# The front of a gated cross-attention and mixture-of-experts kernel, with keys and queries merged into one product of raw inputs

## The reference, cut to what matters

```python
# x (4, 256, 256), ctx (4, 256, 64); 1024 tokens in all
kv   = ctx @ W_k.T + b_k                                   # per batch (256, 64)
out  = einsum('bij,bjd->bid', layernorm(x), kv)            # queries
sim  = einsum('bid,bjd->bij', out, kv) / 16
sim  = (sim - mean) * rsqrt(var + 1e-6) * ln_gamma + ln_beta
x    = x + tanh(g_xattn) * softmax(sim)
h    = layernorm(x)
# router: sigmoid(h @ gate.T), 2 of 4 groups by their two best, 4 of 16 experts, weights normalised * 2.5
x    = x + tanh(g_ffn) * (sum over experts w * (silu(h@gw.T) * (h@uw.T)) @ dw.T  + shared expert)
```

## Time and profile before

| | us |
|---|---|
| median of 3 runs | 198.45 |
| lowest, highest | 196.81, 202.37 |
| the profiled execution | 198.22 |
| its span, first to last instruction | 196.4 |

### The profile page before, as it was taken

The page is one execution under the profiler, slowest core; times in us unless marked ns, Lnnn a source line. Parts: engine busy times, 40 slices in busy tenths (PEclk is TensorE's granted clock), DMA queues, the critical chain, the costliest instruction groups (busy, mean ns, idle before and its releaser), DMA issues.

```text
span 196.4 us, 2883 instructions
## 1 busy us (share of the span) xinstructions
PE 185.1 (94%) x809; PEld 142.9 (73%) x809; DVE 147.1 (75%) x332; ACT 82.6 (42%) x164; POOL 82.6 (42%) x101
## 2 busy tenths in 40 slices
PE   7899799969899999999999989999999999999992
PEld 5565477847588888887788767888888888888871
DVE  0759968999899599998569999856676656666563
ACT  2448724523337833345466343343434343434210
POOL 2352161731832655553336434344445544445300
PEclk9999969999999999999999999999999999999999
DMA  6967200001775446632121000222211122111403
GB/s 154 331 191 228 72 0 0 0 0 34 242 213 176 150 135 164 170 123 53 53 53 53 3 0 18 98 76 76 63 53 53 57 78 76 56 53 53 160 0 110
DMA packets 10264, 18.06 MB, mean 92 GB/s; under 512 B 1741, under 2 KB 3789, under 8 KB 10254
## 3 DMA queue, kind: packets, MB, share of 16 engines
q1 hardware_dynamic: 9760, 17.37, 28.9%
q10 hardware_dynamic: 494, 0.57, 1.3%
HBM read 16.82 MB, written 1.11 MB: 91 GB/s over the span
## 4 chain that ended last, share of the span: by engine, by line
PE 69%; DVE 18%; DMA 6%; ACT 2%; issue 2%; DVEq 0%; POOL 0%; SPq 0%
PE bank L792 40%; PE bank L836 21%; DMA xs<-x_in 3%; DVE act_hi L556 2%; DVE act_lo L564 2%; DMA w_row<-weight_rows 2%; DVE bank L559 2%; PE bank L869 2%; PE bank L739 2%; PE bank L722 1%; DVE stats L461 1%; DMA weight_rows<-w_blk 1%; DVE beats L600 1%; PE bank L762 1%; PE bank L805 1%
## 5 line engine op out<-in xcount | busy, mean ns | idle before, releaser
L281 POOL TENSOR_TENSOR w_lo<-w_raw,w_hi 128x256 fp32r<-128x256 f32 (+1 forms) x72 | 72.0, 1018 | 77.3 <-ACT w_hi L324 76.3
L324 ACT CAST w_hi<-w_raw 128x256 fp32r<-128x256 f32 (+2 forms) x72 | 36.5, 513 | 55.5 <-PE bank L836 29.5
L792 PE MATMUL bank<-hT_hi,w_hi 128*128 128x512 f32 x142 | 56.5, 398 | 0.0
L792 PE MATMUL bank<-hT_lo,w_hi 128*128 128x512 f32 x142 | 56.3, 397 | 0.0
L792 PE MATMUL bank<-hT_hi,w_lo 128*128 128x512 f32 x142 | 44.6, 396 | 0.0
L538 DVE TENSOR_TENSOR weighted<-bank,w_row 128x512 f32<-128x512 f32 x30 | 20.7, 689 | 25.6 <-ACT bank L383 25.3
L792 PEld LDWEIGHTS bank<-hT_hi,w_lo 128*128 128x128 f32 x142 | 26.7, 188 | 6.4
L792 PEld LDWEIGHTS bank<-hT_hi,w_hi 128*128 128x128 f32 x142 | 26.7, 188 | 6.4
L792 PEld LDWEIGHTS bank<-hT_lo,w_hi 128*128 128x128 f32 x142 | 26.7, 188 | 6.1
L383 ACT ACTIVATE bank<-bank 128x512 f32<-128x512 f32 x30 | 17.5, 582 | 27.5 <-PE bank L792 27.5
L564 DVE TENSOR_TENSOR act_lo<-bank,act_hi 128x512 fp32r<-128x512 f32 (+1 forms) x37 | 25.0, 677 | 3.6
(11 more groups left out here) (104 smaller groups left out, 139.7 us busy)
## 6 DMA issues: line engine op xcount, KB each, us to landing
w_row<-weight_rows SPq DMA_DIRECT2D x31, 256.0 KB, 3.2
w_raw<-w_in SPq DMA_DIRECT2D x18, 384.0 KB, 3.8
xs<-x_in SPq DMA_DIRECT2D x4, 256.0 KB, 6.1
out<-x SPq DMA_DIRECT2D x4, 256.0 KB, 2.8
cw<-ctxw_in ACTq DMA_DIRECT2D x1, 276.2 KB
vec<-vecs_in ACTq DMA_DIRECT2D x1, 265.0 KB, 5.9
weight_rows<-w_blk SPq DMA_DIRECT2D x4, 16.0 KB
gw<-route_in ACTq DMA_DIRECT2D x1, 16.0 KB, 6.3
```

Source lines behind the costliest of these rows:

```text
L281: nc.gpsimd.tensor_tensor(w_lo[:, par, cols], w_raw[:, bass.ds(n, 1), cols].rearrange("p o c -> p (o c)"), w_hi[:, par, cols].bitcast(F32) ...
L324: nc.scalar.copy(w_hi[:, par, cols], w_raw[:, bass.ds(n, 1), cols].rearrange("p o c -> p (o c)"))\
L792: last = nc.tensor.matmul(dst, w[:, par, w0 + c * P:w0 + (c + 1) * P], m, start=i == 0, stop=i == len(parts) - 1, skip_group_check=True)
```

## The change: what it does

Queries and keys are no longer formed. With `square` = [W b]^T [W b], the score of a row of x and a context position is, up to the row's own scale and shift (which the normalisation of the scores removes), x times the context rows (`gathered`), times `square`, times the centred context (`projected`). The raw x is loaded a second time, already transposed. `offset` takes the mean key out, `centre_context` centres the context. For batches 0 and 1 GpSimd multiplies u by gamma and TensorE makes a second, scaled score product (`similarity_gamma`); for batches 2 and 3 VectorE multiplies by gamma (`sim_scale`). The variance of x enters only the small constant under the root (`row_eps`). The layer norm of x, its transposes and its copies go. The loads are cut into pieces and reordered. All copies out of PSUM in the front, other than `square`, are on ScalarE. The shared slices' gate and up products are taken batch by batch, those of batch 0 ahead of batch 1's hidden state.

```diff
 # SP
-            for b in range(B):
                 sp.dma_start(xs[:, 2 * b:2 * b + 2, :], x_v[:, 2 * b:2 * b + 2, :]).then_inc(x_in[b], 16)
...
+            load_rows(0, 1, rows0_in)
+            load_xT(0)
+            load_x(0)
+            load_xT(1)
+            load_x(1)
+            load_slice(0, 0)
+            load_slice(1, 1)
+            load_xT(2)
+            load_xT(3)
+            load_x(2)
+            load_x(3)
 # GpSimd
-            for b in range(B):
-                root(0, b)
+            pool.wait_ge(vec_in, 16)
+            u_times_gamma(0)
+            u_times_gamma(1)
+            root(1, 0)
+            root(1, 1)
             pool.wait_ge(gwhi_ready, 1)
...
             low_gu(0, 0, 0)
-            root(1, 0)
-            root(1, 1)
-            pool.wait_ge(scaled_ready, 1)
-            nc.gpsimd.tensor_tensor(x1[:, 3, :], prob[:, 3, :], xs[:, 3, :], ALU.add).then_inc(x1_ready[1], 1)
+            low_gu(1, 1, 1)
             root(2, 0)
             root(2, 1)
             pool.wait_ge(hid_ready[1], 2)
             low_d(0, 0, 0)
-            low_gu(1, 1, 1)
             root(1, 2)
 # ScalarE: queue, then work
-            act.dma_start(cw[:], ctxw).then_inc(ctxw_in, 16)
+            act.dma_start(wk[:], wk_aug).then_inc(wk_in, 16)
+            load_context(0, 1, cT0_in)
+            load_context(1, 2, cT1_in)
+            act.dma_start(rows[:, 1, :, :].rearrange("p c e -> p (c e)"), ctx_rows[:, 1, :]).then_inc(rows1_in, 16)
             act.dma_start(vec[:], vecs.partition_broadcast(P).rearrange("p o v -> p (o v)")).then_inc(vec_in, 16)
+            load_context(2, B, cT_in)
+            act.dma_start(rows[:, 2:B, :, :].rearrange("p b c e -> p b (c e)"), ctx_rows[:, 2:B, :]).then_inc(rows_in, 16)
             act.dma_start(gw[:], route_w.rearrange("(c p) e -> p c e", p=P)).then_inc(gw_in, 16)
...
+            offset_copy(0)
+            r_copy(0)
+            u_copy(0)
+            offset_copy(1)
+            u_copy(1)
+            r_copy(1)
             act.wait_ge(vec_in, 16)
             nc.scalar.activation(gates[:], vec[:, V_GATES:V_GATES + 2], ACT.Tanh).then_inc(gates_ready, 1)
...
+            act.wait_ge(cT_in, 16)
+            centre_context(2)
+            centre_context(3)
             act.wait_ge(gw_in, 16)
             nc.scalar.copy(gw_parts[:, :, 0:E], gw[:]).then_inc(gwhi_ready, 1)
...
+            softmax_exp(0)
+            offset_copy(2)
             high_gu(0, 0, 0, 16, False)
+            r_copy(2)
+            r_copy(3)
+            u_copy(2)
+            offset_copy(3)
+            u_copy(3)
             high_gu(1, 1, 1, 16, False)
             hidden_high(0)
+            softmax_exp(1)
+            high_d(0, 0, 0, False)
             hidden_high(1)
             logitT_copy(0)
             logit_exp(0)
 # VectorE
+            copy_square()
+            centre_context(0)
+            centre_context(1)
             x_stats(0)
+            sim_stats(0)
             x_stats(1)
+            sim_logits(0, 1)
             sim_stats(1)
             attention_scale(0)
             residual(0)
+            x1_stats(0)
+            row_logits(1, 2)
+            normalise(2, 0, 3, x1, hid, hid_ready)
+            row_max(1)
+            hidden_low(0)
             attention_scale(1)
+            residual(1)
             x1_stats(1)
+            x_stats(2)
+            normalise(2, 1, 4, x1, hid, hid_ready)
             sim_stats(2)
+            sim_scale(2)
             hidden_low(1)
+            x_stats(3)
             add_logits(0)
             score_groups(0)
 # TensorE
+            keep_warm(5, bank[7])
+            squared()
+            keep_warm(5, bank[7])
+            offset(0)
+            gathered(0)
+            projected(0)
+            keep_warm(2, bank[7])
+            offset(1)
+            projected(1)
+            similarity(0)
+            gathered(1)
             keep_warm(3, bank[7])
+            similarity_gamma(0)
+            similarity(1)
+            offset(2)
+            similarity_gamma(1)
+            keep_warm(2, bank[2])
+            gathered(2)
+            gathered(3)
+            projected(2)
+            offset(3)
+            projected(3)
+            pe.wait_ge(sim_read[0], 2)
+            keep_warm(4, bank[0])
...
+            pe.wait_ge(r_ready, 3)
             hidden(0)
+            similarity(2)
+            early_gate(0, 0)
+            early_up(0, 0)
+            early_gate(1, 0)
             hidden(1)
-            first_gate(0)
-            route(0)
+            similarity(3)
+            early_up(1, 0)
 # TensorE, in gate_up, the shared slices (first is 0 or 1)
+                if first < 2:
+                    early_gate(first, 1).then_inc(gate_done, 1)
+                    if first == 0:
+                        route(0)
+                    else:
+                        route_back(0)
+                    early_up(first, 1).then_inc(up_done, 1)
+                    return
```

More of the change, by code:

```diff
@@ L94, in build @@
         rstd = sb("rstd", [P, 3, NT])
[L95 removed]
+        row_eps = sb("row_eps", [P, NT])
         neg_max = sb("neg_max", [P, NT])
@@ L220, in write_rows, with load_x, load_rows, load_xT @@
                     sp.dma_start(rows[c], w_blk[:, h, 32 * c:32 * c + 32]).then_inc(rows_out[c], 16)
-            for b in range(B):
+            def load_x(b):
                 sp.dma_start(xs[:, 2 * b:2 * b + 2, :], x_v[:, 2 * b:2 * b + 2, :]).then_inc(x_in[b], 16)
+            def load_rows(first, last, landed):
+                sp.dma_start(rows[:, first:last, :, :].rearrange("p b c e -> p b (c e)"), ctx_rows[:, first:last, :])\
+                  .then_inc(landed, 16)
+            def load_xT(b):
+                sp.dma_start(xT[:, b, :, :].rearrange("p c t -> p (c t)"), xt[b]).then_inc(xT_in[b], 16)
+            load_rows(0, 1, rows0_in)
[9 more added lines that the diff above has]
+            load_x(3)
             ahead = 8
-            for n in range(ahead):
-                if n >= 2:
-                    sp.wait_ge(w_in[n % 2], 16 * (n // 2))
+            for n in range(2, ahead):
+                sp.wait_ge(w_in[n % 2], 16 * (n // 2))
                 load_slice(n, n % 2)
@@ L703, in _, with squared, offset, projected @@
         def _(pe):
[L704 to L716 removed]
+            def squared():
+                pe.wait_ge(wk_in, 16)
+                nc.tensor.matmul(square_ps[0:CA, 0:CA], wk[:], wk[:], start=True, stop=True).then_inc(square_done, 1)
+            def offset(b):
+                if b < 2:
+                    pe.wait_ge(sum_dve, b + 1)
+                else:
+                    pe.wait_ge(sum_act, b - 1)
+                if b == 0:
+                    pe.wait_ge(square_ready, 1)
+                else:
+                    pe.wait_ge(offset_ready, b)
+                nc.tensor.matmul(offset_ps[0:CA, 0:1], square[0:CD, B, :], ctx_sum[0:CD, b:b + 1], start=True, stop=True)\
+                  .then_inc(offset_done, 1)
+            def projected(b):
+                pe.wait_ge(offset_ready, b + 1)
+                if b < 2:
+                    pe.wait_ge(mid_dve, b + 1)
+                else:
+                    pe.wait_ge(mid_act, b - 1)
+                if b == 2:
+                    pe.wait_ge(u_ready, 2)
+                nc.tensor.matmul(u_ps[b][0:CA, 0:S], square[:, b, :], cT_mid[:, b, :], start=True, stop=True)\
+                  .then_inc(u_done, 1)
+            def gathered(b):
+                pe.wait_ge(xT_in[b], 16)
+                pe.wait_ge((rows0_in, rows1_in, rows_in, rows_in)[b], 16)
+                if b == 1:
+                    pe.wait_ge(u_ready, 1)
+                if b >= 2:
+                    pe.wait_ge(r_ready, b - 1)
+                for c in range(C):
+                    last = nc.tensor.matmul(r_ps[b][0:CA, 0:S], rows[:, b, c, :], xT[:, b, c, :],
+                                            start=(c == 0), stop=(c == C - 1), skip_group_check=True)
+                last.then_inc(r_done, 1)
             def transposes(b, dst, source, ready, done):
@@ L808, in first_gate, with early_gate, early_up @@
                 return last
+            def early_gate(k, b):
+                return early(k, gate_ps[k], 0, b)
+            def early_up(k, b):
+                pe.wait_ge(hTlo_ready[0], 1)
+                if k == 1:
+                    pe.wait_ge(r_ready, 4)
+                return early(k, up_ps[k], C * P, b)
             def gate_up(k, par, half, first):
```

289 lines of the change are left out of this document (125 added, 164 removed).

## The result

The changed kernel takes 203.11 us (median of 4 runs, 202.88 to 204.05), the kernel before 198.24 beside it: ratio 1.0279, interval 1.021 to 1.0348. Forecast was 200.7, a change inside two per cent. The time lies in the range, but it is 4.9 us slower where 2.5 were forecast, and so slower by more than can be put down to the measurement. The profiled execution took 202.88, its span 200.8.

What follows compares the result with a forecast made beforehand. VectorE was taken to set the pace to the router's start, with the end following one for one. 198.22 + 1.7 (router later) + 0.8 (clock dip) = 200.7 us, range 197.0 to 203.6.

Steps and rivals of the forecast that it cites:

- The front: Work up to the first scores' statistics: start at 9.5 in place of 14.16, a gain of 4.6.
- costed at nothing: Items given no cost: `row_eps`, GpSimd's vector wait (vectors by 7), weight slices behind batch 1's x, transposed x of batches 2 and 3.
- The root's wait: On GpSimd, slice 1's `low_gu` stands ahead of the root VectorE needs; VectorE idles 2.3.
- Rival 1: The root does not wait because `high_gu(1)` comes 2.3 earlier: 197.6, or 198 to 199 in between; chance 0.23.
- The router's start: Start of `add_logits`, the router's reduction: 34.1 in place of 32.39, 1.7 later, plus 0.8 for the clock.
- TensorE's stretch: From the end of `hidden_low(1)` to the router's reduction: 3.05 where it was 2.1.
- 0.8 for the clock: TensorE idle from 25.0 to 28.1 ahead of `hidden(1)`; a 3.4 us clock dip there costs 0 to 1.3, taken as 0.8.
- the end moves one for one with the start of `add_logits`: All work from 32.39 on hangs on the router's start, and VectorE's list behind it stays as it is.
- is covered by VectorE: A clock dip behind TensorE's idle 2.7 us after `early_up(1,1)` costs nothing, since VectorE sets the pace there.
- "Same" at 0.74: Chance given to a measured time within two per cent, 4.0 us, of the kernel before; faster 0.06, slower 0.20.
- Rivals 2 and 3: Rival 2: TensorE bounds after router start, 194.1, chance 0.06; rival 3: clock low from `hidden(1)` to transposes back, 204.8, chance 0.11.
- Rival 4: Front gains less, transposed x and its context late; at 2.5 late, 9.5 becomes 12 and the time 203.2; chance 0.10.

Runs made afterwards that it cites:

- the second trace: The changed kernel run and profiled once more with no edit, against the kernel before: ratio 1.0248.
- the kernel with the root first: Changed kernel with GpSimd's first root of the new x moved ahead of slice 1's low part: ratio 1.0257 to the kernel before, median 202.43.
- the gap filled: Changed kernel with ten products of zeros behind the last early up product, in TensorE's second gap: ratio 1.0224 to the kernel before, median 201.87.
- the first trace: The first profiled execution of the changed kernel as it is: 202.88 us, span 200.8.
- the order behind it was made for it: Changed kernel with root first, both gaps filled, route ahead of most early products, batch 1's low part ahead of batch 2's scaling: ratio 0.9934, median 196.34.
- its second trace: The kernel before, unchanged, profiled once more: 197.15 us, span 195.3.

## Why the prediction was wrong, point by point

- **The front.** Forecast 9.5 for the first statistics (9.3 to 11), measured 10.62. The ten idle products were taken at the 0.40 of the earlier trace rows, which held for the first group of five (2.50, with its latency) and mostly for the second, 2.13; but `squared` between them started only at 3.90, and they ended at 6.43, not at 5.6. It did not wait for its weights, which had landed 2.1 after their issue at 0.8. Of what was costed at nothing, the vectors came at 10.0, not by 7, and cost nothing. The first logits, at 13.14, waited 0.26 for the scaled product, but that stood behind `gathered(1)` and three products of zeros in TensorE's own list; in the second trace the vectors came at 9.1, and the wait was 0.26 too.
- **The root's wait** was right: 2.51 measured, 2.3 forecast, in the place named. Rival 1 is out.
- **The router's start** was right in sum, 2.45 of 2.5, with terms that cancel: the front 1.12 late, VectorE from there 0.73 shorter than summed (`hidden_low(1)` ended at 31.44, not 31.05), TensorE's stretch 3.40 in place of 3.05, and no 0.8 for the clock. The fall of the clock came where the root's wait had already made it harmless. That the term is real, only in another place, the kernel with the root first shows: there it takes 1.4.
- **The step that failed** is "the end moves one for one with the start of `add_logits`", and with it the sentence that a dip in TensorE's second gap "is covered by VectorE". VectorE does set the pace there, but its own instructions became longer. The low clock delays gate and up of slice 2, the first expert's; ScalarE's cast of slice 4 waits for those products, and GpSimd's low part for the cast. So `w_lo`, which in the kernel before was over at 42.93, ahead of `picked` at 43.46, now runs beside it. `picked` takes 0.79 and ends at 46.80, 0.08 behind the end of `w_lo` (46.72); `w_tok` takes 0.48 and ends at 48.24, 0.12 behind the next one (48.12). The cost was 0.70 in one execution and 1.09 in the other, and nothing with the gap filled. That is a third of the 2.2 us by which the first trace lies above the forecast, and 1.09 of the 1.8 of the second. By the Trainium skill, SBUF — State Buffer, section "SBUF: two separate sides", VectorE with two inputs in SBUF and a GpSimd instruction that reads SBUF contend for one pair of ports, and whichever starts second waits for the whole instruction of the other: these rows agree, with ends 0.08 and 0.12 apart. The trace of before had the collision too: ahead of `picked`, in the ranks of the groups, and in its second half, where `picked` takes 0.55 in both kernels. Its timeline:

```profile
35.47 4.07 POOL L281 TENSOR_TENSOR w_lo<-w_raw,w_hi 128x512 fp32r<-128x512 f32 x4 [3.32 <-ACT w_hi L324]
...
37.72 1.20 DVE L599 TENSOR_TENSOR ties<-ties,before 128x64 f32<-128x64 f32 x1
...
41.66 1.27 POOL L281 TENSOR_TENSOR w_lo<-w_raw,w_hi 128x512 fp32r<-128x512 f32 x1 [2.11 <-ACT w_hi L324]
...
43.46 0.22 DVE L619 TENSOR_TENSOR picked<-masked,replaced 128x64 f32<-128x64 f32 x1
...
115.14 1.29 POOL L281 TENSOR_TENSOR w_lo<-w_raw,w_hi 128x512 fp32r<-128x512 f32 x1 [2.26 <-ACT w_hi L324]
...
115.96 0.55 DVE L619 TENSOR_TENSOR picked<-masked,replaced 128x64 f32<-128x64 f32 x1
```

- The price of the failed step could thus have been read beforehand: TensorE late by one fall of the clock, and then the question what else, besides TensorE's products, comes later.
- **What is left.** 1.25 in the first trace is the output's transfer, which was not so long in any other trace and has no cause shown, and 0.26 lies outside the span (the changed kernel and its variants have 1.8 to 2.2 there, the kernel before 1.8); I have no cause for that. In the second trace the sum is 2.78 + 1.09 + 0.03 + 0.41 = 4.31, for 202.53. The executions without a trace can't be split so.
- **The chances.** A forecast 2.5 slower lies 1.5 from the bound of two per cent; one surcharge of 0.7 to 1.1 and half a us of spread use that up. "Same" at 0.74 priced only known terms. Rivals 2 and 3 did not come: the first gap's dip was over before `hidden(1)`. Rival 4 came by 1.1 of its 2.5.

## What to carry to other kernels

A gap that a change opens on TensorE has to be costed twice: by where the clock's fall behind it lands, which another wait can shift, and by which casts and low parts come later and whose instructions they then meet on the ports of VectorE and GpSimd. Work taken early is free only if it does not stand ahead of the product that releases the engine which sets the pace: half products that stand ahead of the route and of its transposes back cost 1.4, and the same products behind them nothing. The gain of a shorter front was real (3.5 us) and came through, 2.4 of it at the router's start, only when the order behind it was made for it: 0.9934 of the time before, against 1.0279.

## What the runs showed of the hardware that was not expected

- The front reaches full pace at a time that differs from execution to execution of the same products: behind 6 us in one trace, about 10 in another, about 16 in a third, with 1.00 in the column of the granted clock throughout. The first statistics follow, 10.18 to 12.93.
- A fall of the clock to half lasted 3.4 us in seven of the eight between 20 and 50 us, and 6.8 in one. There, each of the seven idle stretches of TensorE of 2.55 to 2.66 us had one (behind it, or in one case from its midst); of the twelve of 1.1 to 1.8 us one had, in the first trace of the kernel before, and the same stretch in its second trace had none.
- A VectorE operation on 64 columns with two inputs in SBUF takes 0.21 alone and up to 1.34 beside one on GpSimd.
